# Edge attributes loaded in their own order and turned by TensorE, and one of every 64 row gathers moved from GpSimd to SyncE

## The reference: attention along the edges of a graph

```python
E = (edge_attr @ We + be)
score = K[src] * Q[dst] / sqrt(12) * E            # per edge, 96 wide
score = exp(clip(score.sum over each head, -5, 5))  # 8 numbers per edge
msg = V[src] * score
wV, Z = segment_sum(msg, dst), segment_sum(score, dst)
out = layernorm(x + wV / (Z + 1e-6))
```

## Time and profile before

| what | value |
|---|---|
| median of three runs | 4178.64 us |
| the profiled execution, its own time | 4178.04 us |
| its span, first to last instruction | 4176.2 us |
| busy: POOL, PE, DVE, ACT | 75%, 73%, 65%, 34% |
| mean granted clock of TensorE | 0.509 |
| chain that ended last: POOL, "issue" | 62%, 22% |
| gathers on POOL | 3224, 946 ns each |
| DMA packets | 1533399, of which 1392683 under 512 bytes |

### The profile page before, as it was taken

How to read it: one execution, slowest core, us unless ns; L and a number is a source line. 1 busy time by engine, 2 the same in 40 slices (tenths; PEclk the granted TensorE clock), 3 DMA queues, 4 the chain that set the end, 5 groups by cost and what they waited for, 6 DMA issues and landing times.

```text
span 4176.2 us, 61383 instructions
## 1 busy us (share of the span) xinstructions
PE 3048.5 (73%) x16776; PEld 2960.0 (71%) x16777; DVE 2698.4 (65%) x6866; ACT 1402.5 (34%) x3656; POOL 3134.1 (75%) x3361
## 2 busy tenths in 40 slices
PE   7797777777777777777777777777777777777775
PEld 7797677777677677777677677776777677776674
DVE  4786666666666666666666666666666666666666
ACT  3443333333333333333333333333333333333335
POOL 7777777777777777777777777777777777777775
PEclk8555555555555555555555555555555555555555
DMA  9897777777777777777777777777777777777763
GB/s 264 168 156 138 134 133 131 132 134 134 131 130 133 135 133 131 132 133 135 131 130 133 134 134 130 132 134 135 131 131 132 134 134 130 131 134 133 133 123 111
DMA packets 1533399, 570.88 MB, mean 137 GB/s; under 512 B 1392683, under 2 KB 1453788, under 8 KB 1533365
## 3 DMA queue, kind: packets, MB, share of 16 engines
q1 hardware_dynamic: 1369107, 237.47, 37.3%
q0 software_dynamic: 156832, 321.69, 37.3%
q10 hardware_dynamic: 7426, 11.35, 0.8%
HBM read 547.37 MB, written 22.87 MB: 137 GB/s over the span
## 4 chain that ended last, share of the span: by engine, by line
POOL 62%; issue 22%; DVE 5%; DMA 5%; PE 1%; POOLq 1%; DVEq 0%; ACT 0%; ACTq 0%
POOL kv_mem L608 62%; DMA kv_mem<-kv_table,src_idx 5%; DVE kqe L1056 1%; DVE msg_mem L1069 1%; DVE kqe L1053 1%; DVE eaT L1076 1%; PE bank L721 0%; DVE y_stats L1169 0%; POOLq L52 0%; PE bank L732 0%; DVE oh L1065 0%; POOLq L605 0%; DVE raw_score L1060 0%; DVE accT L1050 0%; DVE mean_var L1182 0%
## 5 line engine op out<-in xcount | busy, mean ns | idle before, releaser
L608 POOL DMA_INDIRECT kv_mem<-kv_table,src_idx x3224 | 3049.8, 946 | 991.3 <-issue 971.7
L721 PE MATMUL bank<-w_e,eaT 97*128 97x96 f32 x6448 | 1624.5, 434 | 1057.2 <-DVE eaT L1076 1055.6
L721 PEld LDWEIGHTS bank<-w_e,eaT 97*128 97x128 f32 x6448 | 1446.1, 329 | 1125.1 <-DVE eaT L1076 1114.0
L732 PE MATMUL bank<-oh,msg_mem 128*104 128x32 f32 x6448 | 1258.1, 359 | 6.2 <-DVE msg_mem L1069 6.2
L732 PEld LDWEIGHTS bank<-oh,msg_mem 128*104 128x104 f32 x6448 | 1211.2, 293 | 6.7 <-DVE msg_mem L1069 6.7
L1053 DVE TENSOR_TENSOR kqe<-kv_mem,bank 128x384 f32<-128x384 f32 x806 | 444.5, 551 | 1071.7 <-DMA kv_mem<-kv_table,src_idx 1067.3
L848 ACT ACTIVATE msg_mem<-score 128x32 f32<-128x32 f32 x806 | 184.7, 229 | 2651.8 <-DVE score L1083 2650.0
L854 ACT ACTIVATE away<-off_mem,minus_row 96x512 bf16<-96x512 uint8 x806 | 568.8, 706 | 2.0 <-issue 2.0
L1076 DVE STREAM_TRANSPOSE eaT<-ea_mem 96x512 f32<-96x512 f32 x806 | 564.4, 700 | 0.0
L857 ACT ACTIVATE ohT<-away 96x512 bf16<-96x512 bf16 x806 | 507.2, 629 | 25.4
L1056 DVE TENSOR_TENSOR kqe<-kqe,bank 128x384 f32<-128x384 f32 x806 | 446.2, 554 | 27.8
(11 more groups left out here) (96 smaller groups left out, 509.8 us busy)
## 6 DMA issues: line engine op xcount, KB each, us to landing
ea_mem<-in_edge_attr_dram SPq DMA_DIRECT2D x603, 256.0 KB, 7.8
kv_mem<-kv_table,src_idx POOLq DMA_INDIRECT x3224
off_mem<-offset_by_chunk SPq DMA_DIRECT2D x201, 204.0 KB
q_win<-q_table SPq DMA_DIRECT2D x806, 19.9 KB
kv_table<-kv_mem SPq DMA_DIRECT2D x25, 336.0 KB
q_table<-msg_mem ACTq DMA_DIRECT2D x25, 252.0 KB
x_res<-in_x_dram SPq DMA_DIRECT2D x25, 168.0 KB
out_dram<-kv_mem SPq DMA_DIRECT2D x25, 168.0 KB
```

The costliest lines, as they stand in the source:

```text
L608: pool.indirect_dma_start(kv[:, slot, g, :], None, kv_dram[:, :], bass.IndirectOffsetOnAxis(ap=src_idx[:, u % IDX_RING, g:g + 1], axis=0)) ...
L721: nc.tensor.matmul(e_ps[v][:, g * D:(g + 1) * D], eaT[:, v, g * P:(g + 1) * P], w_e[:, :], start=True, stop=True)
L732: last = nc.tensor.matmul(sums_of(s, v), msg[:, w, g, :], oh[:, w % DEPTH, g, :], start=(g == 0), stop=(g == G - 1), skip_group_check=True)
```

## The change

Four things are edited together.

- Attributes: one DMA per half-round (`load_edges`) loads them as they lie, edge `4p + g` of a chunk on partition p, 1536 bytes in one piece. PE turns them, four transposes of 128x96 per chunk into a PSUM bank (`turn_ps`), three chunks ahead; ACT copies them to `eaT`, two chunks ahead. DVE's transpose goes. The Q products now have two PSUM banks instead of four, and PE waits for `kq_done` of two chunks before.
- Edge order: a chunk's group g is now its edges `4p + g` instead of `128g + p`, so the destination and source tables of the first phase are written in that order (strided reads and writes on POOL and PE there).
- Gathers: in every sixteenth chunk up to chunk 799 POOL gathers three groups instead of four (`gathered`). The fourth group's 128 rows are loaded by SP, one DMA per row into `row_mem`, 32 of them in each half-round (`take_rows`, `load_rows`). SP first reads the 128 source numbers into `row_idx` (`load_row_sources`, one small DMA per 16 chunks), then takes them into registers 16 at a time. A row is cut into four pieces of 192 bytes. DVE handles that group in two more instructions of its own, 128x96 each, in such a chunk.
- `base_tab` is now row 0 of `base_all`, so one small load in the first phase goes. SP's and DVE's loops run over 32 chunks a round instead of 16.

The diff, cut to its core:

```diff
+COPY_LEAD = 2
+Q_DEPTH = 2
+TURN_DEPTH = 2
+ROW_CHUNKS = 16
+BLOCK = 2 * ROW_CHUNKS
+ROW_STEP = 32
+ROW_LOAD = 16
...
-                for k in range(0, D, SQ):
-                    engine.dma_start(ea[k:k + SQ, slot:slot + chunks, :].rearrange("i c (b f) -> i (c b) f", f=SQ),
-                                     edge_attr[bass.ds(edge, chunks * CHUNK), k:k + SQ].rearrange(
-                                         "(b i) f -> i b f", i=SQ)).then_inc(ea_in[g], 16)
+                engine.dma_start(ea[:, slot:slot + chunks, :, :].rearrange("p c g d -> p c (g d)"),
+                                 edge_attr[bass.ds(edge, chunks * CHUNK), :].rearrange(
+                                     "(c p g) d -> p c (g d)", p=P, g=G)).then_inc(ea_in[g], 16)
...
+        def gathered(s, u):
+            return G - 1 if u % ROW_CHUNKS == ROW_CHUNKS - 1 and (not isinstance(s, int) or s < WHOLE) else G
...
+        def load_rows(engine, first, last, place):
+            for p0 in range(first, last, ROW_LOAD):
+                nodes = nc.values_load_multi_w_load_instructions(
+                    row_idx[0:1, place, p0:p0 + ROW_LOAD], engines=(engine.engine,), min_val=0, max_val=N - 1,
+                    skip_runtime_bounds_check_because="sources are numbers of nodes")[1]
+                for r, node in zip(range(p0, p0 + ROW_LOAD), nodes):
+                    engine.dma_start(row_mem[r:r + 1, place, :].rearrange("a (r d) -> a r d", r=4),
+                                     kv_dram[bass.ds(node, 1), :].rearrange("a (r d) -> a r d", r=4)).then_inc(rows_in[place], 16)
...
+            def take_rows(s, u):
+                if isinstance(s, int) and s >= WHOLE:
+                    return
+                place, phase = u // ROW_CHUNKS, u % ROW_CHUNKS // HALF
+                if phase == 0:
+                    sp.wait_ge(row_idx_in[place], ...)
+                    sp.sem_inc(rows_allowed, 1)
+                    at_least(sp, msg_ready, s - ROW_CHUNKS)
+                    sp.sem_inc(rows_allowed, 1)
+                load_rows(sp, phase * ROW_STEP, (phase + 1) * ROW_STEP, place)
+                if phase == ROW_CHUNKS // HALF - 1:
+                    ...
+                        load_row_sources(sp, chunk, place)
...
             def half_round(s, h, bases, u):
...
                     load_edges(sp, t, h)
+                take_rows(s, u)
...
-                for g in range(G):
+                for g in range(gathered(s, u)):
                     pool.indirect_dma_start(kv[:, slot, g, :], None, kv_dram[:, :],
...
+                    at_least(pe, ea_turned, t - TURN_DEPTH + 1)
+                    for g in range(G):
+                        last = nc.tensor.transpose(turn_ps[w % TURN_DEPTH][0:D, g * P:(g + 1) * P], ea[:, w, g, :], ident[:, :])
+                    last.then_inc(ea_flipped, 1)
...
+                    act.wait_ge(ea_flipped, k + 1)
+                    nc.scalar.copy(eaT[0:D, (u + COPY_LEAD) % DEPTH, :], turn_ps[(u + COPY_LEAD) % TURN_DEPTH][0:D, :]).then_inc(ea_turned, 1)
...
-                    nc.vector.transpose(eaT[0:D, w % DEPTH, :], ea[:, w, :]).then_inc(ea_turned, 1)
```

More of the change, by code:

```diff
@@ L269, in gnn_kernel @@
         kv_in = [sem(f"kv_in{i}") for i in range(KV_RING)]
+        row_idx_in = [sem(f"row_idx_in{i}") for i in range(2)]
+        rows_allowed = sem("rows_allowed")
+        rows_in = [sem(f"rows_in{i}") for i in range(2)]
         pe_step = sem("pe_step")
+        columns_made = sem("columns_made")
+        ea_flipped = sem("ea_flipped")
         ea_turned = sem("ea_turned")
@@ L449, in load_queries, with half_round @@
                 sp.dma_start(q_win[:, u, :], q_dram[bass.ds(base * PARTS, SEL_READ), :]).then_inc(q_win_in[u // HALF], 16)
[L451 removed]
+            def take_rows(s, u):
[3 more added lines that the diff above has]
+                if phase == 0:
+                    sp.wait_ge(row_idx_in[place], (s - u) * (16 // BLOCK) + 16 if isinstance(s, int) else block_now[0] * 16 + 16)
+                    sp.sem_inc(rows_allowed, 1)
[3 more added lines that the diff above has]
+                if phase == ROW_CHUNKS // HALF - 1:
+                    chunk = s - phase * HALF + 2 * ROW_CHUNKS + ROW_CHUNKS - 1
+                    if not isinstance(s, int) or chunk < WHOLE:
+                        load_row_sources(sp, chunk, place)
+            block_now = [0]
+            def half_round(s, h, bases, u):
                 sp.wait_ge(pe_step, s - HALF)
@@ L746, in add_queries @@
                     last.then_inc(f_q_added, 1)
+                taken(pe, f_ea_in, 16)
+                for g in range(G):
+                    last = nc.tensor.transpose(turn_ps[0][0:D, g * P:(g + 1) * P], ea[:, 0, g, :], ident[:, :])
+                last.then_inc(f_flipped, 1)
                 taken(pe, f_turned)
@@ L866, in further @@
             def further(c, extra):
+                taken(act, f_flipped)
+                nc.scalar.copy(eaT[0:D, 0, :], turn_ps[0][0:D, :]).then_inc(f_turned, 1)
                 taken(act, f_score_ready)
@@ L984, in repeated_away @@
                 dve.wait_ge(node_id_ready, REL_PIECES)
[L987 to L990, removed]
+                nc.vector.memset(rel[0:DUP // G, FULL * G:C * G], NOWHERE).then_inc(node_id_ready, 1)
+                dve.wait_ge(node_id_ready, REL_PIECES + 1)
             for b in range(1, BATCHES + 1):
```

140 lines of the change are left out of this document (87 added, 53 removed).

## The result

The changed kernel takes 4669.29 us (median of four runs, 4667.06 to 4672.43) against 4178.87 for the kernel before in the same session: ratio 1.1172 [1.1158, 1.1186]. Forecast: 4657. The profiled execution took 4670.3 us, its span is 4668.5, the granted clock 0.509 as before.

What follows compares the result with a forecast made beforehand. POOL bound the old kernel; SP becomes the bound: 16.2 us added against 13.9 available makes 22.0 us a half-round instead of 20.0. With the start at 160.6, 199 half-rounds and the end, 4657 us, 11.5% more; range 4200 to 4915.

Steps and rivals of the forecast that it cites:

- POOL's gathers bound the kernel before, 1.253 us each: POOL set the old kernel's pace; 50 gathers fewer by 1.253 us take 62.7 us off POOL.
- 5.55 us of SP go with the attribute loads: On SP, two of three attribute DMAs go in each half-round, freeing 5.55 us.
- PE 3.5 to 4.75 us a chunk, hidden; ACT's copy hidden; strided reads nothing: PE's transposes fit under POOL's 4.92 us a chunk; ACT's 576 ns copy hidden; first-phase strided reads taken as 0.
- A row load 0.44 us (0.42 to 0.48): On SP each single-row load takes 0.44 us, near a Q load; 32 make 14.1 us a half-round.
- A read of 16 numbers 0.98 us with its surroundings: On SP, reading 16 source numbers into registers takes 0.98 us, extrapolated from one and eight numbers; twice 2.0 us.
- The Q stall stays: On SP's queue the four Q loads keep their 2.4 us stall in each half-round, whatever the attributes do.
- Two waits and the load of source numbers, 0.1 us: On SP these come once in four half-rounds and were counted as 0.1 us in the half-round's sum.
- Nothing else on SP's path: SP's added sum was rows, register reads, waits and source-number load, 16.2 us a half-round, with no further term.
- The end: First half-round at 160.6 us, 184 by 22.0, 15 by 23.0, then last rows, six chunks and 71.8 us: 4657 us.
- the first: Rival: SP keeps up, half-rounds under 19.3 us, POOL stays the bound, 4116 us; chance 14%.
- The second: Rival: the Q stall goes with the attributes' small pieces, half-rounds of 19.6 us in the loop, 4215 us; chance 6%.
- The third: Rival: each row load stalls like a Q load in a series, 0.68 us, 29.7 a half-round, 6190 us; chance 5%.

Runs made afterwards that it cites:

- run 8: Changed kernel with one turn of SP's loop covering 64 chunks instead of 32: 4610.61 us, ratio 1.1042.
- run 2: Kernel before, keeping its attribute loads and DVE's transposes, plus SP's row loads at the end of each half-round: 5727.87 us, ratio 1.3709.
- run 5: Changed kernel with SP's order altered: offsets, attributes, then each Q load followed by eight row loads: 4314.98 us, ratio 1.0329.
- run 3: Changed kernel with one of 128 groups moved to SP instead of one of 64, 16 rows a half-round: 4146.01 us, ratio 0.9925.
- run 7: Kernel of run 6, but chunk 15 keeps its four gathers on POOL, so SP's first 128 row loads fall away: 4114.32 us, ratio 0.9849.
- run 1: Changed kernel with the attributes' part alone: POOL gathers all groups, SP loads no rows: 4177.64 us, ratio 1.0002.
- run 4: Changed kernel with each row load written as one piece instead of four, which changed no transfer: 4668.6 us, ratio 1.1175.
- run 6: Kernel of run 5 with the chunk loop's offsets and attribute loads issued by ACT instead of SP: 4162.55 us, ratio 0.9964.

## Why the prediction was right

The mechanism, the sign and the size held. The kernels of the family in which SP is the bound differ in time as the mean distance of SP's half-rounds says (for run 8 over the same 184 half-rounds):

| kernel | half-round, us | time, us |
|---|---|---|
| rows alone (2) | 27.51 | 5727.87 |
| the change | 22.21 | 4669.29 |
| longer loop (8) | 21.89 | 4610.61 |
| rows between Q loads (5) | 20.28 | 4314.98 |

From the change to run 2 it is 5.30 x 199 = 1055 us (measured 1059), as the written-out half-rounds grow too; to run 5 it is 1.93 x 184 = 355 (measured 354), as those stay at some 22 us.

By the prediction's own steps:

- *POOL's gathers bound the kernel before, 1.253 us each.* Right: runs 3 and 7 regained that price for 25 and 49 of them.
- *5.55 us of SP go with the attribute loads.* Right: 5.6 in run 1, 5.3 in run 2.
- *PE 3.5 to 4.75 us a chunk, hidden; ACT's copy hidden; strided reads nothing.* Right: run 1; the copy is 574 ns. Without a wait PE's chunk now takes 4.21 us, its first products starting at 2300.72 and 2304.93:

```profile
2300.72 1.86 PE L790 MATMUL bank<-w_e,eaT 97*128 97x96 f32 x8
...
2304.07 1.07 PE L812 MATMUL bank<-ident,ea_mem 128*96 128x128 f32 x4
2304.93 1.86 PE L790 MATMUL bank<-w_e,eaT 97*128 97x96 f32 x8
```

- *A row load 0.44 us (0.42 to 0.48).* At the lower bound: 0.42 on average, 13.5 us for 32 instead of 14.1. The price of the one-row load of `base_tab` was the nearer neighbour, not the Q load's.
- *A read of 16 numbers 0.98 us with its surroundings.* Too low: 1.21 alone, and two rows with a read between them start 1.69 apart instead of 0.42, so 1.27. Two are 2.5 us instead of 2.0. The straight line through one and eight numbers did not hold up to sixteen.
- *The Q stall stays.* Right, a little smaller: 3.60 us in the half-round shown, 3.94 before. Runs 1, 2 and 5 show that it is the Q loads' own spacing, with or without the attributes' pieces. The counts of engines that the prediction worked out by the Trainium skill ("DMA: Bandwidth & Descriptors", section "Why a DMA increments its semaphore by 16 and not by 1") no row shows, and for the row loads it started from four pieces that were one (run 4). The series of twelve Q loads carries the argument without them.
- *Two waits and the load of source numbers, 0.1 us.* Too low: a half-round with that load is 1.2 us longer than its like without, 0.3 on the mean.
- *Nothing else on SP's path.* Wrong: the loop's turn, 4.2 us in 22 of the 184 half-rounds, 0.5 on the mean, was no term of the sum. Without it the half-round is 21.7, 0.3 under the forecast; with it 22.21.
- *The end.* Loop 184 x 0.21 = 39 us over, the first half-round at 157.1 instead of 160.6 (3.5 under), the 15 written out at 22.2 instead of 23.0 (12 under), and from the last row to the end 92 us instead of 102 (10 under): +13, from 4657 to the profiled 4670. So part of the agreement is errors that cancel.
- *POOL waits at its ring's end, DVE for SP's rows.* Right: 610.1 and 1186.4 us.

The rivals: the first (SP keeps up under 19.3 us) was wrong for this kernel, but its threshold held: at 19.40 (run 6) POOL set the pace from 500 us on. Its argument on the late start also held: there it decided 50 us. The second fell with runs 1 and 2. The third fell with the longest of 6400 row loads, 293 ns; its count of four pieces a row was wrong, but one piece only adds to the argument against it.

## What to carry to other kernels

Work moved off the bound onto an idle engine gains only while the receiver's in-order sum, every address, register read and stall included, stays under the pace; past that point each further item is paid for in full. Where the sum is nearly full, look for stalls that other work can fill: rows between the Q loads were worth 354 us, while the moved gathers themselves can bring at most 63. And an early delay counts even when the later pace suffices, if what it holds up is the bound.

## What the runs showed of the hardware

- SP issues a load of one row (768 bytes, one packet), address from a register, every 0.42 us; the DMA instruction is 0.23 of it. A Q load of 106 packets that doesn't stall takes hardly longer, 0.24.
- Four Q loads in a row held SP's queue for 3.1 to 3.9 us in the half-rounds shown, instead of some 1.5 without a stall; with eight row loads between two of them each took 0.23 to 0.25 in the stretch shown (run 5).
- A register read on SP's queue took 0.71 us for eight numbers and 1.21 for sixteen.
- A turn of SP's loop made its half-round 4.2 us longer at 32 chunks a turn and 2.4 at 64 (the change and run 8); SP stood 2.4 to 2.7 us behind the branch in both, and 0.12 in the kernel before with 16 chunks a turn.
- The gathers took 946 ns each with 410013 DMA packets in the run as with 1533399: relief for the DMA engines did not make POOL faster.
